# Tail of a four-batch attention and feed-forward kernel: the bias row of y becomes one 256-wide product ahead of its operand, and 15 filler products stand behind y instead of 19

## What is computed

```python
def _L0_attn_ref(x, Wq, bq, Wk, bk, Wv, bv, Wl, bl, Wo, bo):
    ...
    q = (x @ Wq + bq).reshape(b, t, H, hd).transpose(0, 2, 1, 3)
    k = ((x @ Wk + bk) @ Wl + bl).reshape(b, t, H, lhd).transpose(0, 2, 1, 3)
    v = ((x @ Wv + bv) @ Wl + bl).reshape(b, t, H, lhd).transpose(0, 2, 1, 3)
    attn = jax.nn.softmax(jnp.einsum('bhqd,bhkd->bhqk', q, k) * scale, axis=-1)
    out = jnp.einsum('bhqk,bhkd->bhqd', attn, v)
    out = out.transpose(0, 2, 1, 3).reshape(b, t, L)
    return out @ Wo + bo
...
x = x + _layernorm(_L0_attn_ref(_layernorm(x), ...))
x = x + _layernorm(_L0_ffn_ref(_layernorm(x), ...))
# _L0_ffn_ref: r = sigmoid(xr @ W_r.T); k = relu(xk @ W_k.T)**2; r * (k @ W_v.T),
# where xr and xk mix each token with the token before it
```

## Time and profile before

| what | us |
|---|---|
| median of the three runs shown | 276.54 (273.62 to 278.18) |
| the profiled execution, its own time | 275.95 |
| its span from the first to the last record | 274.2 |
| share of the span in which TensorE is busy | 92% |
| share in which VectorE is busy | 79% |
| mean granted TensorE clock of the execution (1 is 2.4 GHz) | 0.967 |
| start of the products y in the tail | 250.52 |
| start of the first filler | 254.75 |
| start of the first transpose of x1h | 261.11 |

### The profile page before, as it was taken

The page is one execution under the profiler, slowest core; times in us unless marked ns, Lnnn a source line. Parts: engine busy times, 40 slices in busy tenths (PEclk is TensorE's granted clock), DMA queues, the critical chain, the costliest instruction groups (busy, mean ns, idle before and its releaser), DMA issues.

```text
span 274.2 us, 4821 instructions
## 1 busy us (share of the span) xinstructions
PE 252.3 (92%) x1379; PEld 98.3 (36%) x1379; DVE 217.5 (79%) x382; ACT 179.9 (66%) x351; POOL 102.1 (37%) x230
## 2 busy tenths in 40 slices
PE   7764988999999999999999999999999998998980
PEld 3432542232323253233332432333334323334460
DVE  2499889788878889988998899889989898633645
ACT  1435668787787776677777777767776876891042
POOL 4458575110101014552217156521180663307412
PEclk9799799999999999999999999999999999999596
DMA  4344646222020203030302120202021000000001
GB/s 115 115 115 151 172 141 175 70 76 63 28 89 4 87 4 86 2 90 3 86 4 86 40 86 19 69 7 81 2 86 41 2 3 0 4 1 29 9 2 38
DMA packets 13430, 15.64 MB, mean 57 GB/s; under 512 B 2914, under 2 KB 11107, under 8 KB 13411
## 3 DMA queue, kind: packets, MB, share of 16 engines
q1 hardware_dynamic: 12834, 15.15, 18.7%
q10 hardware_dynamic: 576, 0.26, 0.4%
HBM read 11.01 MB, written 4.19 MB: 55 GB/s over the span
## 4 chain that ended last, share of the span: by engine, by line
PE 75%; DVE 10%; DMA 5%; ACT 3%; issue 3%; POOL 1%; SPq 1%; POOLq 0%; DVEq 0%; ACTq 0%
PE psO L1257 21%; PE psB L1245 20%; PE psA L1226 18%; DVE mx L916 4%; PE psM L1150 3%; PE psM L1156 3%; PE psA L1137 2%; PE psB L1379 2%; DMA KS<-k_scr 1%; DVE er L979 1%; DMA x_all<-in_L_attn_x_dram 1%; PE psO L1169 1%; DMA q_scr<-qp 1%; ACT pT L774 1%; DMA k_scr<-kp 1%
## 5 line engine op out<-in xcount | busy, mean ns | idle before, releaser
L916 DVE TENSOR_REDUCE mx<-psA 128x2 f32<-128x1024 f32 x128 | 150.8, 1215 | 25.0 <-PE psA L1226 24.4
L774 ACT ACTIVATE pT<-psB 128x512 f32<-128x512 f32 x244 | 132.6, 597 | 37.8 <-PE psB L1245 36.9
L1245 PE MATMUL psB<-QS,KS 75*128 75x512 bf16 x244 | 92.6, 383 | 1.3 <-DMA QS<-mmT 0.6
L1226 PE MATMUL psA<-KS,QS 72*128 72x512 bf16 x256 | 89.1, 384 | 4.4 <-DMA KS<-k_scr 3.0
L1257 PE MATMUL psO<-pT,Vg 128*32 128x512 f32 x512 | 68.2, 604 | 0.4
L1245 PEld LDWEIGHTS psB<-QS,KS 75*128 75x128 bf16 x244 | 23.2, 97 | 78.7 <-ACT pT L774 58.8
L1226 PEld LDWEIGHTS psA<-KS,QS 72*128 72x128 bf16 x256 | 24.9, 99 | 26.2 <-DVE mx L916 6.6
L489 POOL TENSOR_TENSOR mm<-mx,one 128x16 bf16<-128x16 f32 x16 | 3.4, 216 | 39.4 <-DVE mx L916 39.4
L1257 PEld LDWEIGHTS psO<-pT,Vg 128*32 128x32 f32 x512 | 10.2, 108 | 21.3 <-issue 16.5
L528 POOL TENSOR_TENSOR Vg<-v_st,one 128x128 f32<-128x128 f32 x16 | 6.2, 397 | 28.0 <-PE psO L1257 28.0
L1137 PE MATMUL psA<-warm 128*128 128x512 bf16 x36 | 12.4, 517 | 1.2 <-DVE warm L890 1.2
(11 more groups left out here) (177 smaller groups left out, 284.2 us busy)
## 6 DMA issues: line engine op xcount, KB each, us to landing
QS<-q_scr SPq DMA_DIRECT2D x16, 288.0 KB
KS<-k_scr SPq DMA_DIRECT2D x48, 96.0 KB
q_scr<-qp SPq DMA_DIRECT2D x12, 128.0 KB, 2.3
k_scr<-kp SPq DMA_DIRECT2D x12, 128.0 KB, 2.3
x_all<-in_L_attn_x_dram SPq DMA_DIRECT2D x4, 256.0 KB, 3.2
out_dram<-out_sb SPq DMA_DIRECT2D x3, 256.0 KB, 2.3
QS<-mmT SPq DMA_DIRECT2D x16, 12.0 KB
out_dram<-out_sb SPq DMA_DIRECT2D x2, 128.0 KB, 1.8
```

The source lines that it names most:

```text
L774: nc.scalar.activation(pT[:, n % 2, i, :], score_bank(n, i, last), ACT.Exp, scale=SCALE).then_inc(e_rdy, 1)
L916: nc.vector.tensor_reduce(out=mx[:, g % 2, c:c + 2], in_=psA[:, u, :, :], axis=AX.X, op=ALU.max).then_inc(a_max, 1)
L1226: score = nc.tensor.matmul(psA[:, u, j, :], QS[g][0:ROWS, h, P * t:P * (t + 1)], KS[g][0:ROWS, h, :], start=True, stop=True)
L1245: nc.tensor.matmul(score_bank(n, i, last), KS[g][0:KEXP, i, P * t:P * (t + 1)], QS[g][0:KEXP, i, :], start=True, stop=True).then_inc(b_rdy, 1)
```

## The change

The wait for `w_cen` moves ahead of the transposes of `oq`. The bias row of y is no longer a product for each tile behind the tile's own product. It is one product for each half, 256 columns wide, whose moving operand reads the same 128 bias values twice (`broadcast_to`) and which opens the accumulation. It is issued right behind the transposes "oT" of its half, so that TensorE's order is: transposes of half 0, bias of half 0, transposes of half 1, bias of half 1, y of half 0, y of half 1. The tile products then accumulate on it. Behind them stand 15 fillers instead of 19. ScalarE's, VectorE's, GpSimd's and the DMA queues' instructions stay as they are.

```diff
             for u in range(2):
                 pe.wait_ge(z_o, u + 1)
                 z_transposes(u, "on", lambda t: o_sb[:, P * t:P * (t + 1)], z_on)
+            pe.wait_ge(z_c, 6)
+
+            def z_bias_y(u):
+
+                nc.tensor.matmul(z_bank["y"][u][:, z_cols(u)], ones_row[:, :],
+                                 w_cen[0:1, 1, :].unsqueeze(1).broadcast_to([1, HALF, E]),
+                                 start=True, stop=False)
+
+            def z_product_y(u):
+                for t in z_tiles(u):
+                    last = nc.tensor.matmul(z_bank["y"][u][:, E * t:E * (t + 1)],
+                                            oT[:, P * t:P * (t + 1)], w_cen[:, 0, :],
+                                            start=False, stop=(t == z_tiles(u)[-1]))
+                last.then_inc(z_yp, 1)
+
             for u in range(2):
                 pe.wait_ge(z_oq, u + 1)
                 z_transposes(u, "oT", lambda t: oq[:, t, :, :].rearrange("p h d -> p (h d)"), z_oT)
-            pe.wait_ge(z_c, 6)
+                z_bias_y(u)
             for u in range(2):
                 pe.wait_ge(z_oTc, u + 1)
-                z_product_by_tile(u, "y", (lambda t: oT[:, P * t:P * (t + 1)], w_cen[:, 0, :]),
-                                  (lambda t: ones_row[:, :], w_cen[0:1, 1, :]), ready=z_yp)
-            keep_warm(19)
+                z_product_y(u)
+            keep_warm(15)
```

## The result

The changed kernel has a median of 273.88 us over 20 executions (272.15 to 278.24); the kernel before, 276.41 us over 20 (273.04 to 278.99). The ratio is 0.9941 with a 95% interval of 0.9914 to 0.9969, which is 0.9 to 2.4 us less: clear of noise, and well under the 3.9 us that were forecast. (The ratios here leave out the executions that are more than 1.5% above the fastest of their own kernel, 7 of 20 before and 4 of 20 after, and 19 to 21 of the 35 of before that stand beside e1 to e8; over all executions the medians differ by 2.5 us.) The profiled execution took 275.03 us, its span is 273.2.

A forecast was written before the change was run, and what follows sets the result against it. TensorE's chain through y and 19 fillers, partly at low clock, was taken to bound the tail. Shorter y and fewer fillers, less y's late start, gave a 3.9 us shift: 276.54 - 3.9 = 272.6 us, range 270.5 to 275.9.

The forecast's parts named there:

- the shift of 3.9 us: In the tail, transposes of x1h and all behind them come 3.9 us earlier, between the short- and long-spell cases.
- the late start of y: On TensorE, the bias products ahead of y delay its start by 0.4 to 0.8 us; 0.6 was taken.
- the cost of the clock: Low clock in the tail: shift 4.1 us with a 3.4 us spell, 2.8 with 6.8 us, 4.3 without a fall.
- The loads hidden in y: Without one-partition products between them, eight y records take 0.11 to 0.12 us each instead of 0.207 at full clock.
- The bias products: Two products of 256 columns on TensorE, two records each, at 0.22 to 0.32 us a record, 0.43 to 0.64 a half.
- VectorE and GpSimd: Behind y, GpSimd's scale instead of statistics holds x1 of half 0, which starts 1.95 us earlier (1.2 to 2.15).
- The shift at the full clock: With no clock fall, x1h sets the start of its transposes at 256.8, a shift of 4.3 us.
- the long spell: Low clock for 6.8 us in the tail: the 15 fillers end at 258.1 and the shift is 2.8 us.
- the rival by which the median execution has none: The median execution before had no low clock in its tail; the change brings 1.1 us, 275.4 us; chance 17%.
- The transposes ahead of y: On TensorE, transposes don't count as activity like products, so the clock fall stays; shift 4.1 or 2.8 us.
- The rival with the other sign: Low clock reaches the r and k products, adding 2.9 to 4.9 us: 275.1 to 278.6 us; chance 15%.
- the last step, from the tail to the median: The tail's 3.9 us is taken whole off the median of the runs shown: 276.54 - 3.9 = 272.6 us.

The follow-up runs named there:

- e1: The changed kernel with 19 fillers behind y instead of 15: 275.29 us, ratio 0.9992 to before.
- e8: The changed kernel run once more, unaltered, on another chip: 275.13 us, ratio 0.9981 to before.
- e4: The kernel before, same y order and 19 fillers, with its bias product on 128 rows instead of one: 272.68 us, ratio 0.9896.
- e3: The changed kernel with its two bias products issued where TensorE waits for VectorE: 273.15 us, ratio 0.9899 to before.
- r4: The changed kernel with bias products on 128 rows in waits, 20 fillers behind y, 2 behind x1h's transposes, tail run twelve times: 613.3 us, mean tail 19.07.
- r6: The changed kernel with four more fillers in TensorE's waits ahead of y, tail run twelve times: 631.8 us, mean tail 20.76.
- r7: r6 with 21 fillers behind y instead of 15 and 2 behind the transposes of x1h: 629.1 us, mean tail 20.21.
- e6: The changed kernel with four more fillers in TensorE's waits ahead of y: 275.31 us, ratio 0.9955 to before.
- r2: The changed kernel with its tail run twelve times in one execution: 630.6 us, mean tail 20.73.
- r1: The kernel before with its tail run twelve times in one execution: 665.7 us, mean tail 23.54.
- r5: The kernel before with five more fillers in TensorE's waits ahead of y, tail run twelve times: 643.9 us, mean tail 21.26.
- r3: The changed kernel with 21 fillers instead of 15 and 2 behind x1h's transposes, tail run twelve times: 637.9 us, mean tail 21.19.

## Why the prediction was wrong

The step that failed is the shift of 3.9 us in the sum. Two of its terms were mis-sized, the late start of y and the cost of the clock; with them as measured, 2.8 us are left in the tail. And the sum took the tail's shift one for one into the time, where the ratio shows 1.6 us; why the rest is missing stays open.

**The loads hidden in y: right.** Eight y records at (1.16 - 0.28)/7 = 0.126 us, and e4 shows the cause that was named, the one-partition products.

**The bias products: the first term that was mis-sized.** The range was 0.22 to 0.32 a record, measured 0.31, at its upper edge. The prediction gave each half's transposes 0.22 us; with a one-row product behind them they hold TensorE for 0.34 and 0.37 (252.31 to 252.65, and 253.27 to 253.64). Y's start slipped by 0.96 us against the transposes, beyond the 0.4 to 0.8 that the bounds gave, where 0.6 was taken. Counted in the tail it slipped by 1.06 (2.46 to 3.52). e3 takes the products off the path and gets 0.82 of it back.

**VectorE and GpSimd: right in kind.** GpSimd's scale holds x1, as forecast. x1 of half 0 starts 1.34 us earlier in the tail (6.15 against 7.49) instead of 1.95, which follows in the main from the late y.

**The shift at the full clock: 3.65 instead of 4.3.** `x1h` is what the transposes wait for, as forecast, and it comes 0.65 us later than forecast because of the late y.

**The clock: the second term that was mis-sized.** The sum took one execution of before, with the long spell, and allowed 0.4 us for the clock in all (3.9 of a possible 4.3). The kernel before was read rightly: ten of twelve tails of it have the long spell, so the rival by which the median execution has none falls. But its mean (23.54) is 0.25 under the profiled tail (23.79). The changed tail has a low clock around y in nine of twelve, three of them the long spell that the sum took for the exception, and pays 0.55 in the mean (20.73 against 20.18). Together that is 0.8 instead of 0.4, and 2.8 us of the 3.9 are left: 2.82 by the tails, 2.9 by the whole times.

The transposes ahead of y, which one sentence of the prediction took for a reason that the fall stays, do not bring it by themselves. The same transposes stand ahead of y in r4, r6 and r7, with work in the waits around them, and in none of those 36 tails did the clock fall around y.

**The rival with the other sign happened, at a lower price.** Two of the single profiles with the changed y and 15 fillers (e8, and e6 with filled waits) have the low clock on r and k. r6 and r7 point to the cause: 15 fillers at the full clock end 1.5 us ahead of `x1h`, the idle time that the prediction had computed and given to a rival. The price was put at 2.9 to 4.9 us, for all of those products; the spell covers 3.4 us of time and costs 1.7. So both theory and rival hold, in different executions.

**What stays open: the last step, from the tail to the median.** The prediction took the tail's gain one for one into the time (276.54 - 3.9). Of the tail's 2.8 us the ratio shows 1.6 (0.9 to 2.4), so at least 0.4 us are missing. The medians differ by 2.5 us, and by 2.35 in e8 on another chip, nearer to the tails; the size of the rest is itself uncertain. The low clock on r and k is one candidate for it, at 1.7 us for each execution that has it, but one of two profiles is no frequency, and r2's twelve had none. Another is the draw of spells ahead of the tail, which moved the two profiled executions by 2.7 us against each other. No run separates the two.

## What to carry to other kernels

A product of one partition between products of 128 costs its neighbours their hidden weight loads: give it 128 rows (a tile of 1/128 against the repeated row), and issue it in a wait. A block of fillers has a length that is right for one clock only: at the low clock it is in the way, at the full clock it can end early and the next products may pay. In r4 and r7 TensorE also had work (fillers, or the bias products) in its waits ahead of y and behind the transposes of `x1h`; there the clock never fell where it cost time, and a block of 20 or 21 did no harm. And where spells of low clock fall by chance, repeat the changed stretch a dozen times in one execution before a sum is made from one profile.

## What the runs showed of the hardware

- The fall of the clock in the tail of before was not y's doing alone: it came in twelve of twelve tails (r1), and with five fillers (1.1 us of work) in and around waits of 0.2 to 0.6 us in five of twelve (r5).
- Spells in the tail last 3.4 or 6.8 us, and how much one-row work was still to come at the low clock goes with it. With the changed y and order (r2, r3, e1) those that began up to 3.1 us into the tail, with most of the second bias product still to run, were long, and those from 3.2 us on short. With the y of before they were long up to 5.0 us (r1) and short from 5.0 (r5) and 5.8 (r1) on. With the bias products out of the way (e3) a spell that began at 2.9 was short. Why is not shown.
- Where a spell falls decides what it costs. With 10.2 us of low clock ahead of it, all before 32 us, the tail starts at 248.2 to 249.5 (e1 to e4); with 10.2 us of which 6.8 lie between 44 and 51 us it starts at 250.7 (the changed kernel's profile); with 6.8 us before 31 us at 248.1 (before).
- Whole times of one kernel spread by 3 to 12 us. The tails of one version repeat to 0.03 us where the clock is at its full level throughout, but for the eighth tail of r3, r4, r6 and r7, which is 0.3 us longer; there VectorE starts the second f 0.3 us late with no wait that the profile names.
